# Graph network kernel: where the attention loops take the row numbers of a tile's edge sources from, and how places are loaded

## What is computed

```python
# additive attention (4 heads of 32)          # GAT (2 heads of 128)
projected = (x @ W).reshape(N, HEADS, OUT_CH)   # xl = h @ Wl + bl ; xr = h @ Wr + br
src, dst = projected[row], projected[col]       # e = leaky_relu(xl[src] + xr[dst], 0.2)
scores = einsum('ehc,hc->eh', tanh(src + dst), att)
scores = exp(scores - max(scores))              # softmax over the edges of a node
out = segment_sum(src * scores, col)            # out = segment_sum(xl[src] * alpha, dst)
out = out / segment_sum(scores, col)
```

## Time and profile before

| what | us |
|---|---|
| median of three runs | 5501.65 |
| lowest, highest | 5496.47, 5505.3 |
| span of the profiled execution (first to last instruction) | 5497.5 |
| PE, DVE, POOL, ACT busy in the span | 4273.2, 2919.0, 2977.8, 1550.3 |

### The profile page before, as it was taken

The page is one execution under the profiler, slowest core; times in us unless marked ns, Lnnn a source line. Parts: engine busy times, 40 slices in busy tenths (PEclk is TensorE's granted clock), DMA queues, the critical chain, the costliest instruction groups (busy, mean ns, idle before and its releaser), DMA issues. The chain is left out here.

```text
span 5497.5 us, 98636 instructions
## 1 busy us (share of the span) xinstructions
PE 4273.2 (78%) x23503; PEld 2392.8 (44%) x23606; DVE 2919.0 (53%) x8445; ACT 1550.3 (28%) x4119; POOL 2977.8 (54%) x3246
## 2 busy tenths in 40 slices
PE   5599565787777886357777777776379999999969
PEld 5233333444444443234444444443145555555534
DVE  5899123222222224634554455445667777777757
ACT  0333113233333332322222222221222222222216
POOL 0071124665666564555555555554268888888850
PEclk9999786667777666677888888886589999999989
DMA  2122332222222221133333333331045555555540
GB/s 69 35 74 86 99 99 68 55 56 55 55 55 55 55 56 30 45 96 87 88 91 88 91 89 88 90 91 36 1 94 96 95 95 96 95 95 96 95 90 12
DMA packets 446823, 404.65 MB, mean 74 GB/s; under 512 B 153527, under 2 KB 391942, under 8 KB 446438
## 3 DMA queue, kind: packets, MB, share of 16 engines
q0 software_dynamic: 151904, 198.72, 18.1%
q1 hardware_dynamic: 294790, 204.57, 13.3%
HBM read 315.22 MB, written 87.79 MB: 73 GB/s over the span
## 5 line engine op out<-in xcount | busy, mean ns | idle before, releaser
L939 POOL DMA_INDIRECT gathered<-table,idx x1088 | 1028.7, 946 | 803.1 <-issue 282.5
L1601 POOL DMA_INDIRECT sums<-gathered,idx x606 | 1068.1, 1763 | 245.1 <-issue 172.7
L1463 PE MATMUL bank<-wide 128*128 128x512 bf16 x3533 | 834.2, 381 | 8.3 <-issue 8.3
L939 POOL DMA_INDIRECT wide<-table,idx x528 | 499.4, 946 | 363.7 <-issue 137.8
L1367 DVE TENSOR_SCALAR onehot_t<-dst_row,iota_w,always 64x512 bf16<-64x512 bf16 x606 | 249.3, 411 | 745.8 <-DMA dst_row<-local_rows 716.6
L1788 ACT ACTIVATE msg<-bank,neg_top 80x512 f32<-80x512 f32 (+1 forms) x404 | 275.3, 682 | 1175.6 <-DVE neg_top L1832 714.7
L1463 PEld LDWEIGHTS bank<-wide 128*128 128x128 bf16 x3636 | 323.5, 98 | 381.3 <-issue 3.0
L1721 PE MATMUL bank<-zact,att_cells 128*80 128x512 f32 x404 | 326.9, 904 | 112.6 <-ACT zact L1782 99.3
L1187 POOL TENSOR_TENSOR acc<-acc,msg 128x20 f32 x404 | 176.4, 437 | 423.7 <-issue 201.5
L1700 PEld LDWEIGHTS bank<-ident,gathered 128*128 128x128 f32 x1632 | 239.6, 175 | 359.5 <-issue 330.2
L1830 DVE TENSOR_REDUCE neg_raw<-bank 80x1 f32<-80x512 f32 (+1 forms) x404 | 274.1, 678 | 196.1 <-remote 88.3
(11 more groups left out here) (355 smaller groups left out, 7280.6 us busy)
## 6 DMA issues: line engine op xcount, KB each, us to landing
dst_row<-local_rows SPq DMA_DIRECT2D x606, 64.0 KB
zact<-in_src_flat SPq DMA_DIRECT2D x202, 192.0 KB
edge_rows<-in_attr_rows SPq DMA_DIRECT2D x202, 128.0 KB
gathered<-table,idx POOLq DMA_INDIRECT x1088
counts<-wide SPq DMA_DIRECT2D x4, 3000.0 KB
counts<-fm_ab SPq DMA_DIRECT2D x4, 3000.0 KB
wide<-counts SPq DMA_DIRECT2D x4, 3000.0 KB, 11.0
fm_ab<-counts SPq DMA_DIRECT2D x4, 3000.0 KB, 11.6
```

Of the source, the lines that this page charges most:

```text
L939: pool.indirect_dma_start(out=g[:, j, :], out_offset=None, in_=table, in_offset=bass.IndirectOffsetOnAxis(ap=k.idx[t.slot][:, j:j + 1], ax ...
L1463: pe.matmul(k.bank[b][:, :], k.split[t.two][:, c, :], k.source_hot[t.two][:, b * CHUNK:(b + 1) * CHUNK], start=first, stop=c == PARTS - 1, ...
L1601: pool.indirect_dma_start(out=k.sums[j], out_offset=bass.IndirectOffsetOnAxis(ap=k.idx[t.slot][:, j:j + 1], axis=0), in_=out_rows(t)[:, j, ...
```

## The change

**Source numbers.** All source numbers (128 x 808, 3232 bytes of each partition) are held in SBUF as `sources`. They are fetched once, by one more transfer at the head of SP's part of the `project` stage "proj" (`fetch`). Until then the place holds the first layer's two weight matrices and a bias. In the attention loops VectorE copies a tile's four columns from `sources` into the ring `idx`, as the last step of its round and for tile s, while its other steps get two more rounds of lag. This copy waits for `sums_ready` of tile s-6. GpSimd waits for this copy alone (`idx_ready`), and no longer for `sums_ready` and a transfer. SP's transfer of `idx`, and its four waits for landed gathers, are gone.

**Places.** SP works by pairs of tiles: one value load for two bases, one wait for `z_ready`, one transfer that brings the places of two tiles (128 KB, rows of 2 KB), and the two window transfers.

**Small parts.** `over_tiles` counts rounds right for lags above six. `load_sources` reads `sources` in place of its own transfer. The bias columns share one tensor, and the input `src_rows` is no longer made.

```diff
@@ load_everything
+    k.dst_pair = [k.sb(f"dst_pair{i}", [HROWS, 2 * TILE], BF16) for i in range(DEEP // 2)]
+    k.dst_row = [k.dst_pair[i // 2][:, i % 2 * TILE:(i % 2 + 1) * TILE] for i in range(DEEP)]
...
+    k.sources = k.sb("sources", [P, T * SUB], I32)
@@ project, SP
+                for to, held_in in fetch:
+                    sp.dma_start(to, held_in).then_inc(fetched, 16)
@@ gather
-    pool.wait_ge(idx_loaded[t.slot], (t.rounds + 1) * 16)
+    pool.wait_ge(idx_ready, t.t + 1)
@@
+def load_pair(k, sp, table, ends, dst_loaded, win_loaded, pair):
+    width = table.shape[2]
+    sp.dma_start(k.dst_pair[pair.slot][:, :],
+                 k.local_rows.rearrange("(p two) e -> p (two e)", two=2)[bass.ds(pair.t, 1), :].to_broadcast(
+                     [HROWS, 2 * TILE])).then_inc(dst_loaded[pair.slot], 16)
+    for i, at in enumerate(ends):
+        slot = 2 * pair.slot + i
+        sp.dma_start(k.window[slot][0:WROWS, 0:width],
+                     table[bass.ds(at, WIN), :, :].rearrange("n c f -> (n c) f")).then_inc(win_loaded[slot], 16)
@@ attend, SP
-                def indices(t):
-                    load_indices(k, sp, idx_loaded, rows_loaded, t)
-                def loads(t):
-                    at = window_base(k, sp, t)
-                    wait_count(sp, z_ready, t.t + 1 - DEEP)
-                    load_window(k, sp, table_dst, at, dst_loaded, win_loaded, t)
-                over_tiles(sp, k.tiles, [(0, indices), (2, loads)], head=2, ring=DEEP)
+                def loads(pair):
+                    ends = window_bases(k, sp, pair.t * 2, 2)
+                    wait_count(sp, z_ready, pair.t * 2 + 2 - DEEP)
+                    load_pair(k, sp, table_dst, ends, dst_loaded, win_loaded, pair)
+                over_tiles(sp, k.tiles // 2, [(0, loads)], head=2, ring=DEEP // 2)
@@ attend, GpSimd
-                    wait_count(pool, sums_ready, t.t + 1 - DEEP)
@@ attend, VectorE
+                def indices(t):
+                    wait_count(dve, sums_ready, t.t + 1 - DEEP)
+                    dve.tensor_copy(k.idx[t.slot][:, :],
+                                    k.sources[:, bass.ds(t.t * SUB, SUB)]).then_inc(idx_ready, 1)
...
-                    over_tiles(dve, k.tiles, [(3, tops), (0, onehots), (5, keep_sums), (1, leaky),
-                                              (3, best_of_nodes), (3, edge_weights)], head=2, ring=DEEP)
+                    over_tiles(dve, k.tiles, [(5, tops), (2, onehots), (7, keep_sums), (3, leaky),
+                                              (5, best_of_nodes), (5, edge_weights), (0, indices)],
+                               head=2, ring=DEEP)
...
-                    over_tiles(dve, k.tiles, [(0, onehots), (2, tops), (3, edge_weights)], head=2, ring=DEEP)
+                    over_tiles(dve, k.tiles, [(2, onehots), (4, tops), (5, edge_weights), (0, indices)], head=2,
+                               ring=DEEP)
@@ additive_layer, project "proj"
+            late=[(k.node_sums1[1], 0.0)], fetch=[(k.sources[:, :], k.ins["src_edges"])])
```

More of the change, by code:

```diff
@@ L82, in step @@
             slot = (s_slot - lag) % ring
-            rounds = s_round if s_slot >= lag else s_round - 1
+            rounds = s_round if s_slot >= lag else s_round - ceil_div(lag - s_slot, ring)
             t = rounds * ring + slot
@@ L109, in __init__ @@
         self.blocks = ins["x"].shape[1]
-        self.tiles = ins["src_rows"].shape[0]
+        self.tiles = ins["src_flat"].shape[0]
     def sb(self, name, shape, dt=F32):
@@ L273, in load_everything @@
     loads = []
+    k.sources = k.sb("sources", [P, T * SUB], I32)
+    early = k.sources[:, :].bitcast(F32)
+    for i, name in enumerate(("L0_gnn_W1", "L0_gnn_W2", "L0_gnn_b2")):
+        k.w[name] = early[:, i * F:(i + 1) * F]
+    for name in ("L0_gnn_W1", "L0_gnn_W2"):
+        loads.append((k.w[name], ins[name]))
+    loads.append((k.w["L0_gnn_b2"], ins["L0_gnn_b2"].rearrange("(o f) -> o f", o=1).to_broadcast([P, F])))
     def weight(name, src, shape):
@@ L277, in weight @@
         loads.append((k.w[name], src))
-    for name in ("L0_gnn_W1", "L0_gnn_W2", "L1_gnn_W", "L2_gnn_Wl", "L2_gnn_Wr", "L2_gnn_res_W",
+    for name in ("L1_gnn_W", "L2_gnn_Wl", "L2_gnn_Wr", "L2_gnn_res_W",
                  "L3_gnn_k2f_W", "L3_gnn_Wi", "L3_gnn_Wj", "L3_gnn_dense_W"):
@@ L621, in __init__, with project @@
         self.width = weight.shape[1]
-def project(k, name, src, jobs, clears=(), residual=None, late=()):
+def project(k, name, src, jobs, clears=(), residual=None, late=(), fetch=()):
     J, cs = len(jobs), chunks(k.n_nodes)
@@ L760, in _ @@
                 wait_count(sp, kept, 16 * U * sum(job.table is not None for job in jobs))
+                wait_count(sp, fetched, 16 * len(fetch))
                 for i in range(S):
@@ L921, in gathered, with gather @@
         "p (j f) -> p j f", f=width)
[L924 to L933, removed]
-    pool.wait_ge(idx_loaded[t.slot], (t.rounds + 1) * 16)
+def gather(k, pool, table, width, idx_ready, gathers_begun, rows_loaded, t):
+    pool.wait_ge(idx_ready, t.t + 1)
     pool.sem_inc(gathers_begun, 1)
@@ L944, in gather_sems @@
 def gather_sems(st, ring=RING):
-    idx_loaded = [st.sem(f"idx_loaded{i}") for i in range(ring)]
     rows_loaded = [[st.pool_dma_sem(f"rows_loaded{i}_{j}") for j in range(SUB)] for i in range(ring)]
-    return idx_loaded, st.sem("gathers_begun"), rows_loaded
+    return st.sem("idx_ready"), st.sem("gathers_begun"), rows_loaded
 def window_base(k, eng, t):
@@ L1650, in attend @@
     with Stage(k, name) as st:
-        idx_loaded, gathers_begun, rows_loaded = gather_sems(st, DEEP)
+        idx_ready, gathers_begun, rows_loaded = gather_sems(st, DEEP)
         loads_begun, scores_begun, turns_begun = st.sem("loads_begun"), st.sem("scores_begun"), st.sem("turns_begun")
-        dst_loaded = [st.sem(f"dst_loaded{i}") for i in range(DEEP)]
+        dst_loaded = [st.sem(f"dst_loaded{i}") for i in range(DEEP // 2)]
         win_loaded = [st.sem(f"win_loaded{i}") for i in range(DEEP)]
@@ L2464, in load_sources @@
     B, nq = k.blocks, k.tiles * SUB
-    raw = k.scores[:, 0:nq].bitcast(I32)
     k.src_f = k.scores[:, nq:2 * nq]
@@ L2477, in load_sources @@
     with Stage(k, "srcs") as st:
-        loaded = st.sem("loaded")
         places = Locals(st)
@@ L2617 @@
     src_rows[:n_edges], dst_rows[:n_edges] = src, dst
-    arrays["src_rows"] = _np.ascontiguousarray(src_rows.reshape(tiles, SUB, P).transpose(0, 2, 1))
     arrays["src_flat"] = src_rows.reshape(tiles, TILE)
```

31 lines of the change are left out of this document (16 added, 15 removed).

## The result

| | us |
|---|---|
| the changed kernel, median of 4 runs | 5579.46 (5578.39 to 5585.02) |
| the kernel before, 4 runs beside it | 5499.06 (5489.31 to 5505.3) |
| ratio, with its 95% interval | 1.0146 (1.0128 to 1.0164) |
| span of the profiled execution | 5576.7, before 5497.5 |

The forecast was 5625 us, slower; the loss came out as 80 us in place of 123.

What follows compares the result with a forecast made beforehand. Pool's stops between rows of gathers were taken to bound add and gat. Terms +107 + 31 - 15 = +123 on the profiled 5497.5 us gave 5620.5, or 5625 us from the median; range 5560 to 5690, chance 0.42.

Steps and rivals of the forecast that it cites:

- What bounds the loops: Add and gat: Pool's stops between rows of gathers set the pace; other engines' signals come late during a row.
- SP's parts, taken as 0: Index transfer and four waits gone, places by pairs: frees SP time, ends add's waits for places, worth 0 us.
- The push in gat: Gathers start behind VectorE's index copy, 1.2 to 1.3 us later per stop; 165 stops, 215 us in full, half taken: +107.
- The push in add: In add only the copy and a signal on top, 0.3 us at 104 stops: +31 us, between 0 and 62.
- The start of the loops: Fewer tiles gathered before VectorE must wait for PE's first results, shortening the initial wait: -15 us, between 0 and -25.
- The rest: Fetch of `sources`, the transfer before the filter loop and the columns: 0, within 3 us each way.
- Copy and lock: VectorE's copies might shut out GpSimd's transfers through shared ports: 65 us could be added, but nothing near it seen.
- A: Rival, faster: SP's relief lengthens Pool's rows in add to 12 gathers, -81 us; 5250 to 5480, chance 0.26.
- B: Rival: gat's push is absorbed, or cancels against add's gain; about 5500 us, chance 0.08 shared with another rival.
- C: Rival, small gain: gat's stops take their shortest form, 2.9 us between gather starts, up to 80 us; 5470, chance 0.10.
- D: Rival: push in full, +215 us, +62 in add, no gain at the start, longer stops; 5690 to 5780, chance 0.14.

Runs made afterwards that it cites:

- e9: The kernel before with three gathers per tile in place of four, PE working on old data there: 4955.66 us, ratio 0.8990.
- e2: The kernel before with places loaded by pairs of tiles, its index transfers and old trigger kept: 5483.79 us against 5512.58, ratio 0.9951.
- e4: The changed kernel with the index copy two rounds earlier, not waiting for sums; GpSimd waits for the sums itself: 5471.28 us, ratio 0.9929.
- e1: The kernel before with gathers also waiting for VectorE's copied weights of tile s-5, no index copy, no pairs: 5601.79 us, ratio 1.0167.
- e3: The changed kernel with the index copy earlier in VectorE's round, ahead of `edge_weights` (in gat also `best_of_nodes`): 5560.51 us, ratio 1.0084.
- e6: The changed kernel with its index copy and trigger, but places again by one transfer per tile: 5600.96 us, ratio 1.0161.
- e5: The changed kernel with two value loads on VectorE before the index copy, trigger about 1 us later: 5687.37 us, ratio 1.0322.
- e12: The changed kernel again, on another chip, against the kernel before: ratio 1.0142.
- e8: e4 with a value load of GpSimd between the second and third gather of every tile: ratio 0.9944.

## Why the prediction was right, and where its sizes were off

**What bounds the loops** (the stops between rows of gathers set the pace): right in the main. e9 shows that Pool's gathers pace both loops, and gat's 81 us of loss lie beside 84.5 us more of stops. But the length of a stop moves with the rest of the loop (e9). What holds the signals during a row stays open, as the prediction had left it; the runs show only that the trigger decides.

**SP's parts, taken as 0:** wrong. e2 gives 0.5% or 27 us less than the kernel before, and e4, with both reliefs of SP and the old trigger, 0.7% or 39 us. Beside the late trigger less is seen of it: the changed kernel has 1.0146 where the trigger alone has 1.0167, some 12 us, and the intervals overlap. The guess behind the 0, that relief of SP doesn't shorten the stops, holds for most: 694 us of VectorE's waits became 1.6 us, and add stayed at 1261 us. The Trainium skill's rule on where transfers are issued ("DMA: Bandwidth & Descriptors", "Issuing engines are not separate DMA queues") was near: it calls the issue time saved usually small. Here the gain is small, and it is not nothing.

**The push in gat, half of 215 us = 107:** the mechanism was right (e1, e3, e4), and the term came near: 98 us with the trigger alone (e1), 99 to 106 us between e4 and the changed kernel. The 81 us of the result have a gain from SP's relief in them. That it came near is luck. The full size rests on the two places of the earlier trace rows, where the gather starts at the end of the copy of the weights. At the usual stop it started 1.07 us ahead of that end, and now 0.86 us behind, so the push is 1.9 us in place of 1.2 to 1.3. 165 stops by 1.9 us are about 315 us, and a third of them stayed, not half. (At the places of the earlier trace rows by themselves the push is 0.91 us: the sum counted 0.2 us for the semaphores beside Pool's start, but the 0.78 us from the copy's end to the gather hold both.) A part of what came back can be read as the prediction said: rows of eight in gat rose from 28 to 44 and those of four fell from 134 to 103, and fifteen stops less, at 3.4 us each, are about 50 us. The rest is that the stops themselves grew by 0.8 us and not by 1.9.

**The push in add, +31 us:** add as a whole measured 0. The trigger alone gave +9 us (e1), copy and trigger +16 us (e6), the late trigger against e4 9 to 16 us; the pairs took about 6 us off (e2). All of these are near what two profiles of one kernel differ by, so the price is small and not better known. The reading behind it was right: the weights for the first tile of a row were copied long before it, 3.8 us before the gather at the median, over 2.7 us in eight of ten stops. The price lay inside the bounds named, but its shape was not seen: the change's own delay costs little there, and one microsecond more costs 83 us (e5).

**The start of the loops, -15 us:** -9. The seventh tile's gathers begin 40.5 us after the first in add and 43.4 in gat before; 36.0 and 39.0 after. VectorE's wait of 19.2 us at the start of gat became two, of 3.6 and 8.8 us.

**The rest, 0:** add's first gather starts at 867.1 us in place of 871.1, and gat's first 4.5 us later after add's last; a little over the 3 us each way that were named; they cancel. In e12 the two are 869.6 us and 2.0 us, so most of this is how executions differ.

**The sum** by parts, then: the late trigger with all that belongs to it costs about 119 us against e4, where the prediction had 107 + 31 - 15 = 123, and SP's relief gives about 39 us, where it had 0. Together they are the 80 us that were measured. Taken in the other order, the trigger alone costs 92 us (e1) and SP's relief gives only some 12 us beside it; the two are not independent, so neither order is the right one, and in both the 0 for SP is too little. The direction and the cause were right; the trigger's price came out near by two errors that met, a full push taken too small and a share of it taken too large.

**Copy and lock:** the copy itself costs nothing to be seen. e1 without it loses as much as e6 with it, and gathers take 944 and 946 ns at the median as before. In the changed kernel that says little, since Pool stands and waits for most of the copies; e4, where 340 copies run during a gather and slow none, says more. The rule of the Trainium skill on the ports that VectorE and GpSimd share ("SBUF — State Buffer", "SBUF: two separate sides") stands behind the prediction's estimate of 65 us; no run here shows such a cost.

**The clock** was missing from the working. Gat's matmuls are the same 7684, and PE was busy with them 1095 us before and 1168 us now, at a granted clock of 0.82 and 0.78 of full speed. With the trigger alone it was 0.77. In these two PE's matmuls took longer while the stage waited longer, and in e9 both went the other way. That isn't so in every run: e4 and e2 have 0.80 and 0.81 in gat, less than the kernel before, with 1081 and 1073 us of PE's time, and are faster than it. How much of gat's 81 us comes by way of the clock stays open, since no run changed the clock alone.

**The rivals.** A (SP's relief lengthens rows in add) happened in part: 17 rows of twelve gathers, where there were none. But 37 rows of four came with them, and the sum of stops stayed. e2 has the same mix (18 of twelve, 35 of four) without the push, and add is 6 us shorter there, no more than two profiles differ by; so the longer rows exist and are worth little. B's absorption was refuted by the result and by e1. C, all stops of gat in their shortest form, did not come: from a row's last gather to the next one nine in ten stops now take 3.3 us or more, where that form has 2.9. D's full push came near only with the longer delay of e5.

## What to carry to other kernels

When a small job is moved to another engine to save a transfer, look at where in that engine's round it stands: the engine that waits for it now waits for all that stands ahead of it. Here the copy was free and its place cost 1.6% in e6. The same copy two rounds earlier, with the consumer waiting for its own condition, left the gain of the relieved SP to be seen: 0.7% faster than before. Look also at many places before a push is sized from the timeline: the two shown ahead of the prediction belong to the third of the stops where the gathers start latest against the copy. A producer whose place in the ring allows it should be early and wait for nothing new, and the wait that frees the buffer should stay with the engine that needs it.

## What the runs showed of the hardware

GpSimd's gathers of 128 rows take 944 ns at the median in add, where a row is 512 bytes, and 946 ns in gat, where it is 1 KB, 1.25 us apart in both. Copies of 128x4 numbers by VectorE beside them don't lengthen them (e4, 340 times). From the end of VectorE's copy to the gather that waited for it pass 0.78 us.

The granted clock of TensorE in gat, as a share of full speed and averaged over the stage, was 0.77 to 0.82 with four gathers a tile and 0.97 with three. For the same matmuls PE was busy 1183 to 1073 us in the one case and 936 us in the other. Taking 1.25 us of Pool's time out of a tile gave 1.70 us there; that the clock is the reason isn't shown.

A value load of GpSimd between two gathers has no cost that can be told from nothing (e8 has 0.9944, e4 0.9929, and the intervals overlap), as it fits into the 0.3 us between them. Four fills took 0.22 us and moved the gathers apart by only 0.06 us.
